# One transformer layer in fp32 halves on one core: the same instructions in another order on every engine

## The reference

```
x  = x + cross_attention(ctx, layernorm(x), mask)     # 4 heads of 64, keys: 256 latents + 77 context = 333
x  = x + moe(layernorm(x))                            # shared 512 wide, and 8 experts of 128, top 2 of one group of 4
```

## Time and profile before

| | us |
|---|---|
| median of 3 runs | 1293.72 |
| lowest and highest | 1293.66, 1294.25 |
| profiled execution, its own time | 1296.0 |
| its span, first to last instruction | 1294.1 |
| PE busy in the span | 1218.2 |
| DVE busy | 1048.6 |
| ACT busy | 752.5 |
| POOL busy | 539.6 |
| mean granted TensorE clock | 0.989 of full |

### The profile page before, as it was taken

How to read it: one execution, slowest core, us unless ns; L and a number is a source line. 1 busy time by engine, 2 the same in 40 slices (tenths; PEclk the granted TensorE clock), 3 DMA queues, 4 the chain that set the end, 5 groups by cost and what they waited for, 6 DMA issues and landing times.

```text
span 1294.1 us, 29594 instructions
## 1 busy us (share of the span) xinstructions
PE 1218.2 (94%) x10176; PEld 1105.8 (85%) x10176; DVE 1048.6 (81%) x3561; ACT 752.5 (58%) x1733; POOL 539.6 (42%) x477
## 2 busy tenths in 40 slices
PE   3799999999999999999999999999999999999987
PEld 2589888889888888888888888888888888988876
DVE  3778888888888888888888888888888888888875
ACT  3566556666555666556656556656556566555652
POOL 3244454344344344444344444344444344344332
PEclk9799999999999999999999999999999999999998
DMA  4000000000000000000000000000000000000000
GB/s 145 12 12 21 20 20 10 12 21 20 21 20 16 5 21 20 20 20 20 2 21 20 20 20 20 2 21 20 20 20 20 2 21 21 20 20 20 2 9 17
DMA packets 28227, 25.84 MB, mean 20 GB/s; under 512 B 6640, under 2 KB 27536, under 8 KB 28080
## 3 DMA queue, kind: packets, MB, share of 16 engines
q1 hardware_dynamic: 27744, 23.83, 5.8%
q0 software_dynamic: 336, 0.14, 0.2%
HBM read 15.57 MB, written 8.39 MB: 19 GB/s over the span
## 4 chain that ended last, share of the span: by engine, by line
PE 60%; DVE 18%; issue 14%; ACT 7%; POOL 1%; DMA 1%; DVEq 0%; POOLq 0%; ACTq 0%
PE up_ps L261 8%; PE up_ps L263 7%; PE attn_ps L370 7%; PE up_ps L262 7%; PE attn_ps L356 4%; PE attn_ps L261 4%; PE down_ps L261 4%; DVE masked L830 4%; PE attn_ps L262 3%; PE attn_ps L263 3%; ACT relu L662 3%; PE down_ps L262 3%; PE down_ps L263 3%; ACT relu_sb L657 3%; DVE acc L996 2%
## 5 line engine op out<-in xcount | busy, mean ns | idle before, releaser
L1176 POOL TENSOR_TENSOR hid_lo<-relu,hid_hi 128x512 fp32r<-128x512 f32 x192 | 247.3, 1288 | 417.1 <-DVE hid_hi L981 417.1
L261 PE MATMUL down_ps<-down_hi,hid_hi 128*128 128x256 f32 x768 | 236.1, 307 | 5.1 <-issue 3.0
L996 DVE SCALAR_TENSOR_TENSOR acc<-down_ps,route_w,acc 128x256 f32<-128x256 f32 x512 | 221.6, 475 | 13.9 <-PE down_ps L263 13.5
L261 PE MATMUL up_ps<-x_hi,up_hi 128*128 128x256 f32 x768 | 227.7, 296 | 3.4 <-issue 0.4
L262 PE MATMUL down_ps<-down_lo,hid_hi 128*128 128x256 f32 x768 | 216.3, 282 | 0.0
L263 PE MATMUL down_ps<-down_hi,hid_lo 128*128 128x256 f32 x768 | 216.1, 281 | 0.0
L262 PE MATMUL up_ps<-x_lo,up_hi 128*128 128x256 f32 x768 | 216.1, 281 | 0.0
L263 PE MATMUL up_ps<-x_hi,up_lo 128*128 128x256 f32 x768 | 215.7, 281 | 0.0
L617 ACT ACTIVATE probs<-masked,neg_max,q_scale 128x333 f32<-128x333 f32 x256 | 168.3, 658 | 73.7 <-DVE neg_max L837 73.7
L657 ACT ACTIVATE relu_sb<-up_ps 128x512 f32<-128x512 f32 x192 | 114.6, 597 | 105.8 <-PE up_ps L263 99.2
L981 DVE CAST hid_hi<-relu 128x512 fp32r<-128x512 f32 x192 | 124.6, 649 | 56.6 <-ACT relu L662 56.4
(11 more groups left out here) (147 smaller groups left out, 2821.5 us busy)
## 6 DMA issues: line engine op xcount, KB each, us to landing
x_in<-in_x SPq DMA_DIRECT2D x32, 256.0 KB, 2.8
out<-acc SPq DMA_DIRECT2D x32, 256.0 KB, 2.1
c_in<-in_ctx SPq DMA_DIRECT2D x32, 77.0 KB
up_stage<-in_up_t SPq DMA_DIRECT2D x1, 1536.0 KB, 12.9
down_stage<-in_down_t SPq DMA_DIRECT2D x1, 1536.0 KB, 15.3
mask_in<-in_mask SPq DMA_DIRECT2D x32, 9.6 KB, 2.6
w_stage<-in_w_kv SPq DMA_DIRECT2D x1, 512.0 KB, 5.8
w_stage<-in_w_q SPq DMA_DIRECT2D x1, 256.0 KB, 5.0
```

What stands on the lines that cost most here:

```text
L261: nc.tensor.matmul(out_ap, s_hi, m_hi, start=first, stop=False)
L996: nc.vector.scalar_tensor_tensor(acc[:, t, :], down_ps[:, (e + 1) % 2, t * D:(t + 1) * D], route_w[:, t, e:e + 1], acc[:, t, :], ALU.mult, ...
L1176: nc.gpsimd.tensor_tensor(hid_lo[:, p % HID_RING, :], relu2[:, p % 2, :], hid_hi[:, p % HID_RING, :], ALU.subtract).then_inc(hid_lo_done, 1)
```

## The change

Nothing is computed differently, but for the residual sum and its statistics, which go by row halves. On each engine the calls in `step` stand in another order:

- PE: the router goes ahead of up 1; the scores of heads 0 to 3 follow one another, and those of heads 4 to 7; transposes go 0, 1, 2, then 3, then 4, 5, 6 (right behind the first values' products), then 7; down 1 goes ahead of the first values' products; down 5 goes ahead of `spread_inverse`; key chunk 2 goes ahead of the output projection; down 7 goes ahead of the x2 transposes.
- ACT: softmaxes 0 and 1 go ahead of chunk 2's relu, and the later ones and the copies shift with the transposes.
- DVE: hid 1 goes behind the masks of heads 0 to 3; the masks of heads 4 to 7 are closer together, with the router's levels behind them; the first key norm goes ahead of the second layer norm; add 2 and add 3 go behind the second widening, add 5 ahead of `attn_out`.
- POOL: `ln_low` goes ahead of low 5, the first k scale ahead of the second norm's inverse root.
- The output projection writes the first 256 columns of each bank of up_ps, one semaphore count for each half; the q projection, which writes bank 0, gets a wait for the first half's residual sum.

```diff
             def project_q(b):
+                if not (isinstance(b, int) and b == 0):
+                    pe.wait_ge(x1_done, (b - 1) * T + 1)
...
-                    last = split_product(up_ps[:, 1, t * D:(t + 1) * D], (at_hi[:, k, cols], at_lo[:, k, cols]),
+                    last = split_product(up_ps[:, t, 0:D], (at_hi[:, k, cols], at_lo[:, k, cols]),
                                          (w_hi[:, k, 3 * D:4 * D], w_lo[:, k, 3 * D:4 * D]), k == 0, k == FT - 1)
-                if t == T - 1:
-                    last.then_inc(out_ps, 1)
+                last.then_inc(out_ps, 1)
...
                 ffn("up", 0)
-                ffn("up", 1)
                 if experts:
                     router(f)
+                ffn("up", 1)
                 score_pair(b, 0, experts)
+                score_pair(b, 1, experts)
                 ffn("up", 2)
-                score_pair(b, 1, experts)
                 ffn("up", 3)
                 score_pair(b, 2, experts)
+                score_pair(b, 3, experts)
                 ffn("shared", 0)
                 ffn("shared", 1)
-                score_pair(b, 3, experts)
                 transpose_probs(b, 0)
                 transpose_probs(b, 1)
+                transpose_probs(b, 2)
                 ffn("down", 0)
-                transpose_probs(b, 2)
                 transpose_probs(b, 3)
                 ffn("up", 4)
+                ffn("down", 1)
                 probs_times_v(b, 0)
                 probs_times_v(b, 1)
-                ffn("down", 1)
                 transpose_probs(b, 4)
                 transpose_probs(b, 5)
+                transpose_probs(b, 6)
                 ffn("down", 2)
                 ffn("up", 5)
-                transpose_probs(b, 6)
                 ffn("down", 3)
                 if following:
                     transpose_ln(b + 1, experts)
                 transpose_probs(b, 7)
                 ffn("down", 4)
+                ffn("down", 5)
                 spread_inverse(b, following)
                 probs_times_v(b, 2)
                 probs_times_v(b, 3)
                 if following:
                     project_kv(b + 1, 1)
-                ffn("down", 5)
+                    project_kv(b + 1, 2)
                 project_out(b, 0, following)
                 project_out(b, 1, following)
                 if following:
-                    project_kv(b + 1, 2)
                     project_kv(b + 1, 0)
                     project_q(b + 1)
                 ffn("down", 6)
+                ffn("down", 7)
                 transpose_x2(b)
-                ffn("down", 7)
...
-                ffn(1)
                 if experts:
                     router_exp(f, f_first)
+                ffn(1)
+                softmax(b, 0, first)
+                softmax(b, 1, first)
                 ffn(2)
-                for u in range(4):
-                    softmax(b, u, first)
+                softmax(b, 2, first)
+                softmax(b, 3, first)
+                ffn(3)
+                softmax(b, 4, first)
                 pt_out(b, 0, first)
-                ffn(3)
                 pt_out(b, 1, first)
                 pt_out(b, 2, first)
-                softmax(b, 4, first)
+                softmax(b, 5, first)
                 pt_out(b, 3, first)
-                softmax(b, 5, first)
+                softmax(b, 6, first)
                 ffn(4)
-                softmax(b, 6, first)
+                softmax(b, 7, first)
                 pt_out(b, 4, first)
-                softmax(b, 7, first)
                 pt_out(b, 5, first)
+                pt_out(b, 6, first)
...
+            def residual_half(b, t):
+                if t == 0:
+                    dve.wait_ge(x_res_done, b + 1)
+                dve.wait_ge(out_ps, b * T + t + 1)
+                nc.vector.tensor_tensor(x1[:, t, :], up_ps[:, t, 0:D], x_res[:, t, :], ALU.add).then_inc(x1_done, 1)
+                dve.wait_ge(x1_done, b * T + t + 1)
+                nc.vector.bn_stats(stats2[:, t, :], x1[:, t, :]).then_inc(ln2_step, 1)
...
                 high(0)
-                high(1)
                 routing(0)
...
                 mask_scores(b, 0, first)
                 mask_scores(b, 1, first)
-                routing(1, 2, 3, 4, 5, 6)
                 mask_scores(b, 2, first)
                 mask_scores(b, 3, first)
-                routing(7)
                 negate_max(b, 0)
-                routing(8)
-                high(2)
-                routing(9, 10)
+                high(1)
+                routing(1, 2, 3, 4, 5, 6, 7, 8)
                 mask_scores(b, 4, first)
                 mask_scores(b, 5, first)
-                routing(11, 12)
+                high(2)
+                mask_scores(b, 6, first)
+                mask_scores(b, 7, first)
+                negate_max(b, 1)
+                routing(9, 10, 11, 12)
                 if experts:
                     add_shared(f, f_first)
-                routing(13)
-                mask_scores(b, 6, first)
-                mask_scores(b, 7, first)
-                routing(14)
-                negate_max(b, 1)
-                routing(15, 16)
+                routing(13, 14, 15, 16)
...
                 add(0)
                 widen_inverse(b, 0, first)
+                high(4)
                 if following:
                     normalize1(b + 1, False)
                 add(1)
-                high(4)
-                add(2)
-                high(5)
-                add(3)
                 invert_sums(b, 1)
                 widen_inverse(b, 1, first)
+                add(2)
+                add(3)
                 if following:
                     ln_high(b + 1, False)
+                high(5)
                 add(4)
+                add(5)
                 attn_out(b, first)
                 attn_low(b, 0)
                 attn_low(b, 1)
-                add(5)
+                if following:
+                    k_norms(b + 1, 0, False)
+                residual_half(b, 0)
+                residual_half(b, 1)
                 layer_norm2(b, first)
                 if following:
-                    k_norms(b + 1, 0, False)
+                    k_norms(b + 1, 1, False)
                 normalize2(b, first)
                 if following:
-                    k_norms(b + 1, 1, False)
-                if following:
                     k_normalize(b + 1, 0, False)
...
                 low(4)
+                if following:
+                    ln_low(b + 1)
                 low(5)
                 if following:
-                    ln_low(b + 1)
+                    k_scales(b + 1, 0, False)
                 rstd_second(b, first)
                 if following:
-                    k_scales(b + 1, 0, False)
                     k_scales(b + 1, 1, False)
```

More of the change, by code:

```diff
@@ L636, in attn_high @@
                 if not first:
-                    act.wait_ge(out_ps, b)
+                    act.wait_ge(out_ps, b * T)
                 cols = slice(t * P, (t + 1) * P)
@@ L697, in step @@
                     ln_full(b + 1, False)
-                pt_out(b, 6, first)
                 pt_out(b, 7, first)
@@ L1073, in step @@
                 attn_low(b, 1)
-                add(5)
+                if following:
+                    k_norms(b + 1, 0, False)
+                residual_half(b, 0)
+                residual_half(b, 1)
                 layer_norm2(b, first)
                 if following:
-                    k_norms(b + 1, 0, False)
+                    k_norms(b + 1, 1, False)
                 normalize2(b, first)
                 if following:
-                    k_norms(b + 1, 1, False)
+                    k_normalize(b + 1, 0, False)
                 if following:
-                    k_normalize(b + 1, 0, False)
                     k_normalize(b + 1, 1, False)
@@ L1150, in residual @@
                 if not first:
-                    pool.wait_ge(x1_done, b)
+                    pool.wait_ge(x1_done, b * T)
                 nc.gpsimd.tensor_tensor(x_res[:], x_in[:], bout_row[:].unsqueeze(1).to_broadcast([P, T, D]),
```

## The result

The changed kernel takes 1274.88 us (median of 4 runs, 1273.8 to 1276.13) where the kernel before took 1293.99 (4 runs, 1293.66 to 1295.81): a ratio of 0.985, interval 0.9833 to 0.9867. It is faster by 19 us; 51 were forecast. The profiled execution's span is 1273.5 us (before 1294.1).

The account below looks back on a forecast made before the run. PE was taken to bound the kernel, with DVE having little room. A step falling from 38.7 to 37.0 us saves 1.7 over 30 steps, 51 us, giving 1243 us; the range was 1229 to 1281.

Parts of the forecast that it names:

- The floor: PE with every wait gone and fewer visits: a step of 36.5 us, a time of 1228 us.
- the 1.39 of waits: PE's idle time per step before head 2 and 3 transposes, the inverse's transposes and the first up product: 1.39 us.
- the 0.8 of visits: PE's saving per step from fused score pairs and fewer changes between kinds of product: 0.8 us, bounds 0.5 and 1.1.
- DVE's chain to high 3: DVE's work, idle time and holds from the first up product until high 3 starts: 16.7 us.
- By the rates in the rows it isn't in that mode: DVE's x_hat: its measured rate was taken to show it is not in the double-rate mode that GpSimd would hold.
- the 0.98 that x_hat was given: DVE's normalisation ahead of add 1, counted as not held by GpSimd: 0.98 us.
- the 0.36 at down 3: New PE wait at down 3, which needs DVE's add 1: about 0.36 us a step.
- The first rival: GpSimd's low 4 holds DVE's x_hat: add 1 ends 1.2 later, step 38.2, time 1279 us; chance 0.14.
- No x_hat meets a tensor op of GpSimd: Claim that in the old trace x_hat never overlaps a GpSimd tensor op, so no row decides whether it is held.
- Rival 2: GpSimd's holds stack up on DVE between high 1 and add 1: step 39.2, time 1309 us; chance 0.11.
- The tail: End of DVE's work in a step, through x_lo: ends at 36.8, first up product at 36.9, after the step's first.
- Rival 3: A wash: saved PE waits return in full at down 2, down 3 and down 4, 1291 to 1296 us; chance 0.05.

Follow-up runs that it names:

- run 11: Changed kernel with DVE's add 1 ahead of the first norm, high 4 behind the second widening, high 1 between the second and third masks: 1227.55 us, 0.9467.
- run 3: Changed kernel with one more wait on GpSimd: low 4 starts only when x_hat and c_hat are done; 1246.2 us, 0.9611.
- Runs 1, 2 and 4: 1: high 4 behind the norm, changed kernel, 1254.2; 2: high 4 ahead of the norm, kernel before, 1304.29; 4: high 4 behind add 1, changed kernel, 1275.91.
- Run 9: Changed kernel with high 4 behind the first norm on DVE and key chunk 2 behind the output projection again on PE: 1326.99 us, 1.0242.
- run 7: Changed kernel with high 4 between add 1 and the second inverse on DVE, and low 0 ahead of x_res on GpSimd: 1276.47 us, 0.9852.

## Why the prediction was right in its direction and wrong in its size

**The floor held.** The floor was a step of 36.5 and a time of 1228, with every wait gone: run 11 measures 36.5 and 1227.6. So the 1.39 of waits and the 0.8 of visits together were sized rightly (38.70 - 1.39 - 36.5 leaves 0.81; the changed kernel's sum above leaves 0.73). The fused score pairs follow at 0.15 to 0.16.

**DVE's chain to high 3 held.** Forecast 16.7 after the first up product; measured 426.68 - 409.98 = 16.70. One term in it had the wrong address: `biased` is held as said (0.99 for 0.17), but low 2 holds the second negate and not in_group. These are rows of source lines of the kernel after:

```profile
L930 DVE TENSOR_TENSOR biased<-score,gbias x32: 175/995/1004, 74.8 to 1249.4; 128x16 f32<-128x16 f32 x32
...
L839 DVE SCALAR_TENSOR_TENSOR neg_max<-row_max,q_scale x64: 161/165/508, 43.2 to 1220.8; 128x4 f32<-128x4 f32 x64
```

The negate costs 0.35 where I had 0.4 for in_group, so that the sum comes out to the second figure is partly luck. X_hat starts 2.67 later, to the figure.

**The step that failed** is "By the rates in the rows it isn't in that mode", and with it the 0.98 that x_hat was given in the sum for add 1, and so the 0.36 at down 3. The normalisation took 1.71, add 1 came 0.97 later, and down 3 waited 1.44. The rest of that sum stood, as run 3 shows by taking the hold away: 0.47 at down 3 for 0.36, and 1246 for a forecast of 1243. The first rival had it with its place and nearly its size: 38.2 a step and 1279, for 38.02 and 1274.9. It was wrong in its chance, 0.14. The Trainium skill (GPSIMD Engine Reference, Key points) says that GpSimd contends with DVE instructions in a two-port mode or with two SBUF inputs, and its page VectorE: DVE Perf Modes (the perf-mode tier table) counts an fp32 tensor_scalar from SBUF among the faster ones. The trace agrees that it is held and not that it is fast: 256 columns take 399 ns at the least. I took the rate for a proof that the operation does without what is shared. The rows of before spoke against that proof. sig_den is a TENSOR_SCALAR with one SBUF operand too, and it took 0.52 under low 1 (420.62 to 421.91), which my own list of held work has. The same line in the kernel after, free in all steps but one:

```profile
L926 DVE TENSOR_SCALAR sig_den<-exp_neg x32: 166/168/1017, 74.3 to 1248.1; 128x16 f32<-128x16 f32 x32
```

"No x_hat meets a tensor op of GpSimd" was not right either: the second norm's x_hat (448.90 to 449.63 in the kernel before) runs into the inverse root of k_scale, from 449.07, and isn't held (0.73). No row had an x_hat under a low part, which is the case that counts. With every cast and a TENSOR_SCALAR held, the hold was likelier than not.

**The other rivals.** Rival 2 (holds stack up on the way to add 1) needed 1.8 us of added holds; 0.97 came, since low 2 and biased cost what the forecast had. Rival 3 (a wash) had the waits come back at three places; they came back at one. The tail (the end of DVE's work in a step) came in time: run 3's list has no other wait than down 3's that comes 30 times.

**My expectations had the same fault as the forecast** where they missed. Runs 1, 2 and 4 looked at the held instruction and not at what takes its place: the idle time that a cast had filled, the slack behind a chain, the next instruction that comes under the same low part. Run 9 gave a moved product only its own length, and not the three latencies that it covered.

## What to carry to other kernels

After each cast whose consumer runs on GpSimd, ask what DVE does in the next microsecond: put instructions there that weren't held (here operations that read PSUM, and a reciprocal; reductions and statistics from SBUF never came under a low part, so they are untried), and keep from it casts, copies, TENSOR_SCALARs from SBUF such as the normalisation, and element-wise operations with two SBUF inputs, however small. Moving the cast alone moves the hold to the next in line. To price a hold, look at what DVE would wait for behind it (run 7: nothing gained by freeing a cast), and where no row shows an operation under such a neighbour, its rate proves nothing; try the pair before sizing an order on it.

## What the runs showed of the hardware that I had not expected

- An x_hat half takes 407 ns for 256 columns, where a cast takes 0.40 us for 512, and is nevertheless held to 1391 ns, as long as a copy (1.39 for the 0.29 of the widening).
- Size doesn't matter: `biased`, 16 columns, takes 995 ns for 175, and `neg_max`, 4 columns, up to 508 for 165. What counts is how much of GpSimd's operation is left: the hold was that less 0.13 or 0.14 (`biased` 0.82 with 0.96 left, `neg_max` 0.35 with 0.49, the compare in the earlier trace rows 1.12 with 1.25), and for x_hat that less 0.27 (0.97 with 1.24).
- GpSimd's own kind of operation does: under its inverse roots (L1134, 0.70 to 1.64 us, operands of 2 to 8 columns) nothing of DVE was longer than elsewhere in the middle steps. The second norm's x_hat, of the same form as the held one, is the plainest case; rows of DVE and of POOL, kernel after:

```profile
444.97 0.74 DVE L894 TENSOR_SCALAR x_hat<-x,mv,rstd 128x256 f32<-128x256 f32 x2 [0.29 <-POOL rstd L1134]
...
444.90 1.01 POOL L1134 TENSOR_TENSOR k_scale<-k_norm,minus_half 111x4 f32<-111x4 f32 x1
```

  Only hid_lo, ln_lo and x_res hold, all with hundreds of columns. Whether it is their size or their operation was not tried.
